# Linear attention in chunks of 64 with one denominator per token, two of four score banks masked by GpSimd

## The reference

```
q = relu(x @ Wq.T) + EPS      # 16 heads of 8, 256 tokens, 32 sequences
k = relu(x @ Wk.T) + EPS ;  v = x @ Wv.T
kv_cum = cumsum over tokens of k[:, None] * v[None, :]     # 8x8 per head
out = einsum('d,dm->m', q, kv_cum) / (q . cumsum(k) + EPS) # per token and head
x = x + out @ Wo.T
```

## Time and profile before

| | us |
|---|---|
| median of 3 runs | 2021.92 (2021.71 to 2022.61) |
| profiled execution, span | 2016.8 |
| linear attention, first to last instruction of it | 295.09 |
| one of its 32 sequences in the middle | 8.96 |

### The profile page before, as it was taken

The page is one execution under the profiler, slowest core; times in us unless marked ns, Lnnn a source line. Parts: engine busy times, 40 slices in busy tenths (PEclk is TensorE's granted clock), DMA queues, the critical chain, the costliest instruction groups (busy, mean ns, idle before and its releaser), DMA issues.

```text
span 2016.8 us, 66873 instructions
## 1 busy us (share of the span) xinstructions
PE 1789.7 (89%) x27593; PEld 1374.2 (68%) x27593; DVE 1700.4 (84%) x4108; ACT 1081.8 (54%) x2880; POOL 918.8 (46%) x953
## 2 busy tenths in 40 slices
PE   5998999998999688868999999999999999957887
PEld 4887566665888466656777777777777777745666
DVE  5786899998566699957999999999989999867997
ACT  2444333332444466645666666666666666636664
POOL 1000788886000277733444444444444444426886
PEclk9999999999999899978999999999999999988999
DMA  4000000000000000000000000000000000000001
GB/s 120 1 1 1 1 1 2 1 2 1 1 1 1 0 1 1 1 1 3 3 3 3 3 3 4 3 3 3 3 4 3 4 3 3 3 2 1 22 22 43
DMA packets 14606, 14.49 MB, mean 7 GB/s; under 512 B 1440, under 2 KB 12128, under 8 KB 14304
## 3 DMA queue, kind: packets, MB, share of 16 engines
q1 hardware_dynamic: 11104, 8.83, 1.5%
q10 hardware_dynamic: 3200, 1.37, 0.3%
HBM read 6.01 MB, written 4.19 MB: 5 GB/s over the span
## 4 chain that ended last, share of the span: by engine, by line
PE 43%; DVE 40%; issue 8%; ACT 7%; POOL 1%; DMA 1%; DVEq 0%; POOLq 0%; SPq 0%; ACTq 0%
PE acc L515 6%; PE acc L492 6%; DVE arena L620 5%; DVE arena L1290 4%; DVE arena L1282 4%; PE acc L1809 3%; PE acc L1799 3%; DVE arena L615 2%; DVE acc L938 2%; DVE arena L951 2%; PE acc L1821 2%; DVE arena L1321 2%; DVE arena L928 2%; PE acc L801 2%; PE acc L506 2%
## 5 line engine op out<-in xcount | busy, mean ns | idle before, releaser
L1628 POOL TENSOR_TENSOR arena<-arena 128x288 f32<-128x288 f32 (+1 forms) x384 | 269.7, 706 | 461.6 <-ACT arena L1507 380.4
L975 POOL TENSOR_TENSOR arena<-arena 128x960 f32<-128x960 f32 (+2 forms) x74 | 177.6, 2400 | 301.5 <-DVE arena L944 204.8
L1507 ACT ACTIVATE arena<-acc 64x288 f32<-64x288 f32 x384 | 155.3, 405 | 166.6 <-PE acc L1827 86.9
L723 POOL TENSOR_TENSOR arena<-arena,quadcol 128x512 f32<-128x512 f32 x64 | 79.2, 1256 | 240.5 <-DVE arena L590 240.5
L465 ACT ACTIVATE arena<-acc,wib 128x256 f32<-128x256 f32 x256 | 100.3, 474 | 150.9 <-PE acc L506 150.9
L1282 DVE SCALAR_TENSOR_TENSOR arena<-arena,acc 64x256 f32<-64x256 f32 x384 | 161.2, 420 | 14.4 <-PE acc L1827 2.3
L1290 DVE SCALAR_TENSOR_TENSOR arena<-acc,arena 128x288 f32<-128x288 f32 (+1 forms) x384 | 156.3, 407 | 18.1 <-PE acc L1821 10.9
L1821 PEld LDWEIGHTS acc<-arena 64*64 64x64 f32 x3072 | 112.0, 133 | 83.7 <-issue 76.4
L1821 PE MATMUL acc<-arena 64*64 64x72 f32 (+1 forms) x3072 | 136.8, 224 | 35.1 <-DVE arena L1290 29.4
L1799 PE MATMUL acc<-arena 64*64 64x72 f32 x3072 | 138.5, 229 | 16.5 <-DVE arena L1290 11.4
L1061 PE MATMUL acc<-wguT,arena 128*128 128x352 f32 x256 | 106.4, 499 | 48.8 <-DVE arena L928 47.8
(11 more groups left out here) (242 smaller groups left out, 4780.4 us busy)
## 6 DMA issues: line engine op xcount, KB each, us to landing
out_dram<-X SPq DMA_DIRECT2D x3, 1024.0 KB, 5.4
out_dram<-X SPq DMA_DIRECT2D x1, 512.0 KB, 3.2
wi<-in_wiT_dram ACTq DMA_DIRECT2D x1, 256.0 KB, 6.5
wout<-in_woT_dram ACTq DMA_DIRECT2D x1, 256.0 KB, 9.0
out_dram<-X SPq DMA_DIRECT2D x1, 256.0 KB, 2.3
out_dram<-X SPq DMA_DIRECT2D x2, 128.0 KB, 2.5
wqkv<-in_w_qkv_dram ACTq DMA_DIRECT2D x1, 192.0 KB, 9.0
arena<-in_w_down_dram SPq DMA_DIRECT2D x1, 176.0 KB, 4.6
```

What stands on the lines that cost most here:

```text
L975: pool.tensor_tensor(b3(y[k][:, part(u)]), b3(z[k][:, part(u)]), each(small[u % kept][:, 1, blocks(u)]), ALU.mult).then_inc(y_ready, 1)
L1507: act.mul(sq[s][rows, group[1], :], pn[s][other, group[1], 0:MW], 15.0 / (13.0 * size[it]))\
L1628: pool.tensor_tensor(tm[s][:, group[g], cols], pm[s][:, group[g], cols], sq[s][:, group[g], cols], ALU.subtract).then_inc(tm_ready, 1)
```

## The change

The chunk shrinks from 128 tokens to 64 (`CH`), so only half as many scores are computed. A matmul now gives 64 keys by 256 columns, and the two halves of a 128-token tile are laid one below the other in the partitions of a bank: `A[q]` holds all 256 tokens of a sequence, in four banks filled once per sequence instead of twice. `tri` gets a second part of 64 columns, the small triangle twice one below the other. Banks 0 and 1 are masked by DVE, 2 and 3 are copied by ACT and masked by POOL. With four chunks there are three states, each kept as its 32x32 diagonal blocks only.

Denominators are computed per token: `prod` is now the stationary operand against `headcol`, which gives 128 tokens by 16 heads for each tile. ACT adds the constant, DVE inverts 128x32, ACT repeats each value eight times (`expand`), PE transposes (`turn_z`), ACT copies the result (`turned_z`), and `divide` uses it as before. The blanked copies of the values are no longer made by POOL: ACT writes v into a buffer that POOL has set to zero once.

Two changes stand beside this. The two expert feed-forwards share one set of semaphores (the second one counts on from `N0`), and two small copies on POOL at the program's start make the second part of `tri`.

The pieces below are, in this order, `states` and `invert` on DVE, `values`, `expand` and `turned_z` on ACT, `scores` and the two loops of `mix` on PE.

```diff
                 def states(n, s):
                     dve.wait_ge(state_done, n + 1)
-                    dve.tensor_tensor(state[s], st[s], headblk[:, :], ALU.mult).then_inc(state_ready, 1)
+                    dve.tensor_tensor(state[s].rearrange("p c (k d) -> p c k d", d=HD),
+                                      st[s].rearrange("p c (k d) -> p c k d", d=HD),
+                                      quadcol[:, :].unsqueeze(1).unsqueeze(3).broadcast_to([P, NC - 1, NQ, HD]),
+                                      ALU.mult).then_inc(state_ready, 1)
...
-                def invert(n, s, j):
+                def invert(n, s):
                     dve.wait_ge(sum_ready, n + 1)
-                    dve.reciprocal(zr[s][:, cols], zr[s][:, cols]).then_inc(z_ready, 1)
+                    dve.reciprocal(zt[s], zt[s]).then_inc(z_ready, 1)
...
                 def values(n, s):
                     act.wait_ge(kv_done, n + 1)
+                    if n < STREAMS:
+                        act.wait_ge(blank, 1 + STREAMS)
+                    else:
+                        act.wait_ge(num_done, n - STREAMS + 1)
+                    act.copy(vtok[s], kv[s][:, :, D:2 * D])
+                    for j in range(TPB):
+                        ins = act.copy(vd[s][j], kv[s][:, j, D:2 * D].rearrange("p (q k c) -> p k q c", q=NQ, c=HD))
+                    ins.then_inc(v_ready, 1)
...
+                def expand(n, s):
+                    act.wait_ge(z_ready, n + 1)
+                    act.copy(zx[s].rearrange("p j (h c) -> p (j h) c", c=HD),
+                             zt[s].rearrange("p j h -> p (j h)").unsqueeze(2).broadcast_to([P, TPB * NH, HD]))\
+                       .then_inc(zx_ready, 1)
+                def turned_z(n, s):
+                    act.wait_ge(zT_done, n + 1)
+                    act.copy(zr[s], zT[s]).then_inc(zr_ready, 1)
...
+                def scores(n, s):
+                    for j in range(TPB):
+                        pe.wait_ge(qx_ready, n * TPB + j + 1)
+                        for q in range(NQ):
+                            if n and not j and q < NV:
+                                pe.wait_ge(att_ready, (n - 1) * NV + q + 1)
+                            elif n and not j:
+                                pe.wait_ge(raw_ready, (n - 1) * (NQ - NV) + q - NV + 1)
+                            for h, rows in enumerate(half):
+                                mm = pe.matmul(A[q][rows, j * SEQ:(j + 1) * SEQ],
+                                               qkT[buf(n)][quad(q), 1, j * P + h * CH:j * P + (h + 1) * CH],
+                                               qx[s][quad(q), j, :, h * CH:(h + 1) * CH],
+                                               start=True, stop=True, skip_group_check=True)
...
+                    for h in range(2):
+                        c = 2 * j + h
+                        if c:
+                            for q in range(NQ):
+                                pe.matmul(num[s][quad(q), h, j * CH:(j + 1) * CH], state[s][quad(q), c - 1, :],
+                                          qkT[buf(n)][quad(q), 0, c * CH:(c + 1) * CH], start=True, stop=False,
+                                          skip_group_check=True)
                     for k in range(NQ):
+                        for h, rows in enumerate(half):
+                            for q in range(NQ):
+                                mm = pe.matmul(num[s][quad(q), h, j * CH:(j + 1) * CH], vx[s][rows, j, k, quad(q)],
+                                               att[s][rows, q, j * SEQ + k * CH:j * SEQ + (k + 1) * CH],
+                                               start=(c == 0 and k == 0), stop=(k == NQ - 1), skip_group_check=True)
```

More of the change, by code:

```diff
@@ L374, in halfpasses @@
                 for s in R:
-                    yield i * STREAMS + s, s, 1 - s, not (first and s == 0), not (last and s == STREAMS - 1)
+                    yield N0 + i * STREAMS + s, s, 1 - s, not (first and s == 0), not (last and s == STREAMS - 1)
             def v(dve):
@@ L411, in finish @@
                 def finish(n, s):
[L412 removed]
+                    tile = (n - N0) * TPB
                     dve.wait_ge(y_done, n + 1)
@@ L648, in v @@
                 states(0, 0)
-                for n in range(NB + 2):
+                for n in range(0, NB + 2):
                     s, o = n % STREAMS, 1 - n % STREAMS
[L651 to L659, removed]
+                    run, tail, late = 0 <= n < NB, 0 <= n - 1 < NB, 0 <= n - 2 < NB
+                    head, fore = 0 <= n + 1 < NB, 0 <= n + 2 < NB
+                    if run:
+                        mask(n, s, 0)
+                        invert(n, s)
+                    if head:
                         queries(n + 1, o)
                         sums(n + 1, o)
+                    if late:
+                        finish(n - 2, s)
+                    if tail:
+                        divide(n - 1, o)
+                    if run:
+                        mask(n, s, 1)
+                    if head:
                         products(n + 1, o)
                         keys(n + 1, o)
[L664 to L667, removed]
                         states(n + 1, o)
-                    if n < NB:
-                        invert(n, s, 1)
             def a(act):
@@ L706, in a @@
                 turned_x(1, 1)
[L707 removed]
+                for n in range(0, NB + 2):
                     s, o = n % STREAMS, 1 - n % STREAMS
[L709 to L712 removed]
+                    run, tail, late = 0 <= n < NB, 0 <= n - 1 < NB, 0 <= n - 2 < NB
+                    head, fore = 0 <= n + 1 < NB, 0 <= n + 2 < NB
+                    if run:
+                        evacuate(n, s, 2)
+                        denominators(n, s)
+                        evacuate(n, s, 3)
+                    if fore:
+                        norm(n + 2, s)
+                    if run:
+                        expand(n, s)
+                    if head:
+                        values(n + 1, o)
+                    if fore:
                         turned_x(n + 2, s)
[L714 to L716 removed]
+                    if run:
+                        turned_z(n, s)
             def g(pool):
@@ L817, in mix @@
-                    for k in range(NQ):
-                        for q in range(NQ):
-                            mm = pe.matmul(num[s][quad(q), cols], vx[s][:, j, k, quad(q)],
-                                           att[s][:, j * NQ + q, k * P:(k + 1) * P],
-                                           start=(j == 0 and k == 0), stop=(k == NQ - 1), skip_group_check=True)
+                        pe.wait_ge(v_ready, n + 1)
+                        pe.wait_ge(att_ready, (n + 1) * NV)
+                        pe.wait_ge(att_pool, (n + 1) * (NQ - NV))
```

206 lines of the change are left out of this document (113 added, 93 removed).

## The result

| | before | after |
|---|---|---|
| median of 4 runs, us | 2021.82 | 1992.36 |
| ratio | | 0.9865, 95% interval 0.9842 to 0.9888 |
| span of the profiled execution, us | 2016.8 | 1992.1 |
| linear attention in it, us | 295.1 | 272.2 |

The change makes the kernel faster by about 1.4%, 29 us by the medians; 52 were forecast, 1970 us. The stated range held it, 10 us from its upper end; the part of the range that belongs to the forecast itself, 1955 to 1984, did not. The stage is 22.9 us shorter where 52 were expected; the other 1.8 us of the two spans lie outside it.

A forecast was written before the change was run, and what follows sets the result against it. DVE binds linear attention, PE close behind and binding after the change: PE's 6.96 us plus 0.12 of waiting, taken as 7.2, times 32 plus 12.4 gives 242.8, 52 us fewer, 1970 us; range 1953 to 2002, its own 1955 to 1984.

The forecast's parts named there:

- What binds: Linear attention: DVE binds at 8.96 us per sequence, PE close behind at 8.7; relieving DVE hands the bound to PE.
- the ring: Linear attention: masks, scores, mix and queries wait on each other through DVE and PE; forecast had DVE binding, PE close.
- DVE, POOL: Work per sequence in linear attention: DVE falls to 5.2 us of 8.6, POOL to 5.0 of 7.4.
- PE's price: PE's blocks per sequence: 0.85 ns per column and round, plus shape changes of 0.14 or 0.20 us; mix 1.83 us.
- A round stays 58 ns, or a start stays 14.5 ns and eight take 116. I take 58: Mix on PE, eight tiles, 64 columns: price of one round of eight starts, taken as 58 ns.
- The 0.12 us of waiting for finish: PE before values of the next sequence: ready at 2.80 us, DVE's finish ends at 2.92, so 0.12 lost.
- Sum 6.96 us: PE's blocks per sequence, from queries to project, added up before waits; with waiting 7.1, taken as 7.2 us.
- the ends of the stage: Filling and draining linear attention: 8.4 us before, 4 us added, so 12.4 beside 32 sequences of 7.2.
- Starts at 14.5 ns: Rival, mix on PE: each start costs 14.5 ns whatever the tile; 8.0 us per sequence, 1995 us; chance 0.13.
- Small matmuls at 24 ns and more: Rival, mix and states on PE: 24 to 34 ns per instruction, 10.0 to 11.8 us per sequence, 2059 to 2118; chance 0.08.
- Row tiles in turn on one bank: Rival, mix's state parts: row tiles writing one PSUM bank take turns; 8.1 us per sequence, 1999 us; chance 0.07.
- The granted clock: Rival, PE: granted clock falls to half, PE's 7 us become 14, far slower; chance 0.02.

## Why the prediction was right, and where it was off

**What binds: half right.** That DVE's saving hands the bound to PE is shown by the chain and by DVE's idle times. That DVE alone bound the kernel before is not: with 1.2 us less on DVE the ring still took 8.60 us. The change shortens the ring on both engines (half the scores, a third of the masks); that it gets much further for this reason is argued, not tested by itself. DVE's idle time stands where the forecast put it, before queries and before the state's mask.

**DVE, POOL: right.** 5.15 us for 5.2, 4.94 for 5.0. ACT came out lower, 3.7 for 4.3, with no effect.

**PE's price: right but for one term.** "A round stays 58 ns, or a start stays 14.5 ns and eight take 116. I take 58": a block does neither. Its first 32 starts keep the 58 ns, the rest come 12 ns apart after a short pause; 0.79 us instead of 0.60, 0.38 per sequence. The 0.12 us of waiting for finish vanished under it, so an undisturbed sequence takes 7.33 us for 7.2.

**The step that failed: "Sum 6.96 us" was a sum of execution, with instructions always at hand.** Stops at packets and slower stretches bring the mean from queries to queries to 247.7/31 = 7.99 us. 31 times 0.66 over the undisturbed 7.33 is 20 us, most of what is missing; fifteen of the stops above, eleven in mix and four at the turns of x, cost 15.9 of them, counted from start to start. 31 times 0.13 is 4; the ends of the stage took 24.5 us beside 31 sequences where 19.6 were forecast, among them gaps of 0.8 and 1.7 us and the last mix at a granted clock of 0.50, the lower of the two levels (1.2 GHz, from 465 us on, after PE had been busy for 6.95 of the 10 us before). 20+4+5 is the 29 us between 242.8 and 272.2.

**Luck in the hit.** The forecast's own range, 6.8 to 7.6 us per sequence or 1955 to 1984 us, was missed. The stated range held 1992 only because it also took in rivals whose mechanisms were not at work here; none of them was a stop for instructions.

**Rivals.** Starts at 14.5 ns gave 8.0 us and 1995 and came nearest in number, by another mechanism: with a pace alone every sequence would be alike, and in the middle of the stage they range from 7.33 to 8.7. Small matmuls at 24 ns and more are out: 64 instructions take 0.79 us, 12 ns each. So the floor of 25 ns in the Trainium skill, "TensorE: Matmul & The Clock Gate", section "Wait — 56ns, not 53.3ns?", does not hold across tiles here. Row tiles in turn on one bank are out too: the state parts took 0.24 and 0.35 us, as priced without turns. The granted clock stayed at 1.00, its upper level (2.4 GHz), in both sequences shown.

**Left open.** That a gap keeps to a place in the row of instructions is shown, and that it ends 2.2 to 2.9 us after the start of a packet. Stretches that slow down without a gap have the same mark in the trace: six times between 225 and 440 us scores take 1.24 to 1.68 us to the next block instead of 1.05, and the first late start comes 2.0 to 2.6 us after a packet's start. How far ahead PE's instructions are asked for, and what the 1.2 us and more between a packet's end and PE's next start are, no run here separates. The Trainium skill, "Runtime: NRT & Kernel Launch", section "Instruction fetch mechanics", says that instructions are fetched in blocks of 16 KiB, 256 of them, and that the cost of crossing into the next is mostly hidden. The trace agrees on the block (0.36 MB in 22 packets) and not on the cost, 0.5 to 1.7 us in a stretch as dense as mix.

## What to carry to other kernels

Count instructions per microsecond on an engine as well as their durations: where many small matmuls run in parallel, the stretch can be bound by how fast instructions arrive, and "issue" in the idle times, with a packet on the instruction queue 2 to 3 us before its end, is how it showed here. Such gaps move with every instruction added anywhere before, so two kernels that do the same can differ by 27 us; spread dense stretches with long instructions before judging a change. And before pricing a relief, follow the ring of waits: 1.2 us off the busiest engine gave 0.36.

## What the runs showed of the hardware

On this chip PE started matmuls of 64 columns on eight tiles 7.5 ns apart for 32 instructions and then 12 ns apart on the mean; with 32 columns it was 5.3 and 10.5 ns. With instruction packets of 16 KB, a stretch of 304 PE instructions in 2.2 us stopped for 0.5 to 1.7 us, each stop ended 2.2 to 2.9 us after the start of a packet, and repeating 32 instructions per sequence fixed the place of the stop in all of them.
